# Four graph layers on one core: layer 0 loads x a second time, turned, in place of TensorE's transposes, and GpSimd forms the low half

## The chip, the core and the metric

The kernel runs on one core of a Trainium2 chip. The metric is the time of one execution on the device in microseconds; before the change it is 3392.47 us (median of 3 runs, 3390.36 to 3393.5).

## What is computed

Four layers in turn over x of 128 graphs x 64 nodes x 512 features (float32), each `x = layernorm(x + layer(x))`. Layer 0, the one that matters here, is

```python
Wi, Wj = (W[:, :Din], W[:, Din:])
mi = jnp.einsum('bkd,od->bko', x, Wi)
mj = jnp.einsum('bkd,od->bko', x, Wj)
a = adj.astype(x.dtype)
deg = a.sum(axis=1)
out = deg[None, :, None] * (mi + b) + jnp.einsum('ij,bjo->bio', a, mj)
x = _layernorm(x + out)
```

Layer 1 is a graph attention layer with four heads, an output head and a feed-forward part; layers 2 and 3 are attention layers with one head. None of them is touched.

## The kernel before

The 8192 rows of x are cut into T = 64 tiles of 128 rows (two graphs). The kernel has three stages, one after the other: layer 0 over all tiles (lines 276 to 610), the heads and the output head of layer 1, and a last stage that runs the feed-forward part of layer 1 and layers 2 and 3 as a pipeline. Between stages x goes through a scratch tensor in device memory.

Each engine has its own instruction stream, written out by hand with semaphores; every engine takes its instructions strictly in the order written. Products keep nearly float32 precision by splitting each operand into a high half (rounded to the fp32r type) and a low half (the rest): `product` (L41) runs three passes, hi x hi, hi x lo and lo x hi, on line 47. So every operand needs a hi copy and a lo subtraction.

In layer 0, for a tile t:

- SyncE loads `xt` (L378, four buffers) from device memory, and stores the result `x1` (L376). It waits for x1 of tile t before it stores it, and only then issues the load of xt for tile t + XR. It also loads `v_stage` and `a_pair` (L370, L374) for the attention vectors of later layers.
- TensorE turns the four 128x128 blocks of `xt` into the PSUM tile `turn` (`turn_x`, L566), one tile ahead. `products(t, r)` then makes the Wj product (12 passes, `wj_psum`), the Wi product (12 passes, `wi_psum`, two buffers) and the product with the adjacency (`nb_psum`, L589).
- ScalarE copies `turn` to the high half `x0T_hi` (`x_hi`, L464), then copies `wj_psum` to `wj` (L471).
- VectorE forms the low half `x0T_lo` = turn - hi (`x_lo`, L504) for tile t + 1, then z = wi_psum * deg + xb (L526), z = z + nb_psum (L530), the statistics (L204, L211), in odd tiles below 48 two multiply-and-sum instructions over `v_stage` (`junk`, L541), and then the normalised result x1 (L551).
- GpSimd forms xb = xt + db (L427), where db = deg * b0, and after the statistics of the tile two 128x1 instructions, veps and rstd (L215, L222). Between them it loads and splits the weights of layer 1 that stay in SBUF for the next stage: per pair of tiles one load issued from its own queue (L411), `split_hi` (big_hi, L415) and `split_lo` (big_lo, L420). The order in `two` is: load, xb(t), split_hi, rstd(t), xb(t+1), split_lo, rstd(t+1).

The attention vectors are formed in tiles 0 to 47, in groups of 8 tiles. On SyncE and VectorE groups 1 to 3 (tiles 8 to 31) are a loop over register values, the other groups are unrolled; on GpSimd nearly all tiles run in loops of four. GpSimd's first tile waits until db is ready (`setup_step` 7, L407, set on L517); L504 for tile 0 stands on VectorE between the first and the second piece of the split of W.

Of the kernel before, what the change touches and what calls it, by code (L numbers as in the profile page):

```python
# [5 lines left out]
F32 = mybir.dt.float32  # L6
# [6 lines left out]
P = 128  # L13
# [217 lines left out]
def gnn_stack_kernel(nc, x, adj, W0T, b0, Wh, ah, Wo, ao, w1, b1, w2, b2, gamma, beta,  # L231
# [14 lines left out]
    with ExitStack() as top:  # L246
# [29 lines left out]
        with ExitStack() as ctx:  # L276
# [3 lines left out]
            def sem(n):  # L280
                return ctx.enter_context(nc.semaphore(n))

            XR, UN = 4, 4
# [8 lines left out]
            xt = [sb(f"xt{r}", [P, D]) for r in range(XR)]  # L292
            xT = [(sb(f"x0T_hi{b}", [P, KC, P], F32R), sb(f"x0T_lo{b}", [P, KC, P], F32R)) for b in range(2)]
# [11 lines left out]
            turn = [ctx.enter_context(nc.psum_tensor(f"turn0{b}", [P, KC, P], F32)) for b in range(2)]  # L305
# [6 lines left out]
            loaded = [sem(f"loaded{r}") for r in range(XR)]  # L312
            w0_loaded = [sem(f"w0_loaded{b}") for b in range(2)]
# [5 lines left out]
            xT_done, xT_hi_ready, xT_lo_ready, wj_done, wj_ready, wi_done, nb_done = (  # L319
                sem("x0T_done"), sem("x0T_hi_ready"), sem("x0T_lo_ready"), sem("wj_done"), sem("wj_ready"),  # L320
# [9 lines left out]
            def count(t, r):  # L330

                return 16 * (t // XR) + 16 if isinstance(t, int) else 4 * (t - r) + 16
# [14 lines left out]

            @block.sync
            def _(sp):
                sp.dma_start(xt[0][:], rows(x_rows, 0)).then_inc(loaded[0], 16)  # L350
                for g in range(2):
                    sp.dma_start(adj_i[g * NODES:(g + 1) * NODES, :], adj).then_inc(small_loaded, 16)
                for k in range(2 * KC // WP):
                    piece = (k * WP + KC) % (2 * KC) * P
                    ge(sp, w0_lo_ready, k - 1)
                    sp.dma_start(w0f[k % 2], W0T[piece:piece + WP * P, :].rearrange("(c p) n -> p c n", p=P)
                                 ).then_inc(w0_loaded[k % 2], 16)
                    if k == 1:
                        sp.dma_start(db[:], b0.partition_broadcast(P)).then_inc(b0_loaded, 16)
                        for r in range(1, XR):  # L360
                            sp.dma_start(xt[r][:], rows(x_rows, r)).then_inc(loaded[r], 16)

                def step(t, r, q, G):
                    late = isinstance(G, int) and G >= HEADS
                    if q is not None and r == 0:
                        ge(sp, v_part, 2 * q)
                        for k in range(2):
                            a = ((a2d, a2s), (a3d, a3s))[G - HEADS][k] if late else ah[
                                bass.ds(G, 1), k * D:(k + 1) * D].rearrange("a o -> (a o)")
                            sp.dma_start(a_pair[:, k, :], a.partition_broadcast(P)).then_inc(pair_loaded, 16)  # L370
# [14 lines left out]
            def _(pool):  # L385
# [38 lines left out]
                def tile(t, r):  # L424
                    pool.wait_ge(loaded[r], count(t, r))
                    ge(pool, own_ready, t)
                    nc.gpsimd.tensor_tensor(xb[:], xt[r][:], db[:], ALU.add).then_inc(xb_ready, 1)  # L427

                def two(t, r, q, source, k):
# [5 lines left out]
                    tile(t + 1, r + 1)  # L435
# [3 lines left out]
                def four(k, source, before):  # L439

                    for i in range(2):
                        q = 2 * k + i + before
                        two(2 * q, 2 * i, q, source, 2 * k + i)

                four(0, Wh_rows, 0)
                with pool.Fori(1, NQ // 4) as k:
                    four(k, Wh_rows, 0)
                with pool.Fori(0, NQ // 4) as k:
                    four(k, Wo, NQ // 2)

            @block.scalar
            def _(act):
                for k in range(2 * KC // WP):
                    first = (k * WP + KC) % (2 * KC)
                    if k == 0:
                        act.wait_ge(xT_done, 1)
                        nc.scalar.copy(xT[0][0][:], turn[0][:]).then_inc(xT_hi_ready, 1)
# [3 lines left out]
                def x_hi(t, b):  # L461
                    act.wait_ge(xT_done, t + 1)
                    ge(act, wi_done, t - 1)
                    nc.scalar.copy(xT[b][0][:], turn[b][:]).then_inc(xT_hi_ready, 1)  # L464
# [17 lines left out]
            def _(dve):  # L482
# [19 lines left out]
                def x_lo(t, b):  # L502
                    dve.wait_ge(xT_hi_ready, t + 1)
                    nc.vector.tensor_tensor(xT[b][1][:], turn[b][:], xT[b][0][:].bitcast(F32), ALU.subtract  # L504
                                            ).then_inc(xT_lo_ready, 1)

                for k in range(2 * KC // WP):
# [5 lines left out]
                    if k == 0:  # L513
                        x_lo(0, 0)
# [4 lines left out]
                def step(t, r, q, G):  # L519
                    b = r % 2  # L520
                    if not isinstance(t, int) or t + 1 < T:
                        x_lo(t + 1, 1 - b)
# [38 lines left out]
            def _(pe):  # L561
                def turn_x(t, r):
                    pe.wait_ge(loaded[r % XR], count(t, r % XR))
                    ge(pe, xT_lo_ready, t - 1)
                    for c in range(KC):
                        ins = nc.tensor.transpose(turn[r % 2][:, c, :], xt[r % XR][:, c * P:(c + 1) * P], ident[:])  # L566
                    ins.then_inc(xT_done, 1)

# [25 lines left out]
                turn_x(0, 0)  # L594
                pe.wait_ge(adj_T_ready, 1)
                for r in range(UN):
                    turn_x(r + 1, r + 1)
                    products(r, r)
                with pe.Fori(1, T // UN - 1) as g:
                    t = g * UN  # L600
                    for r in range(UN):
                        if r < UN - 1:
                            turn_x(t + (r + 1), r + 1)
                        else:
                            turn_x(t + UN, 0)
                        products(t + r, r)
                for r in range(UN):
                    if r < UN - 1:
                        turn_x(T - UN + r + 1, r + 1)
# [923 lines left out]
```

## Time and profile before

| | |
|---|---|
| median of 3 runs | 3392.47 us (3390.36 to 3393.5) |
| span of the profiled execution, first to last instruction | 3390.5 us |
| TensorE (PE) busy in the span | 3273.9 us, 97% |
| VectorE (DVE) | 2186.4 us, 64% |
| GpSimd (POOL) | 1989.9 us, 59% |
| ScalarE (ACT) | 1691.7 us, 50% |
| device memory traffic | 93.09 MB read, 50.33 MB written |

The profiled execution is one run; the span is shorter than the time measured for a run by what lies around it. Busy time of an engine counts compute instructions only; matmuls are pipelined, so the durations of two that follow each other overlap, and the distance between their starts says what one costs. PEld is TensorE's weight load, SPq SyncE's queue. In a timeline each row is: start in us, duration in us, engine, line, operation, output<-inputs, count, and in brackets how long the engine had been idle before it and what ended that.

### The profile page before, as it was taken

How to read it: one execution, taken by the hardware profiler on the slowest of the kernel's cores; microseconds unless marked ns; L12 is line 12 of the kernel's file. 1: busy time of each engine (PE TensorE's matmuls, PEld its weight loads, DVE VectorE, ACT ScalarE, POOL GpSimd, SP SyncE). 2: the span in 40 equal slices, each digit the busy share in tenths (PEclk: the TensorE clock that was granted, in tenths of full speed). 3: DMA queues.
4: the chain of work that ended last, by engine and by line, in shares of the span. 5: the costliest groups of instructions: out<-in, count | busy, mean ns of one | idle time of the engine just before them, and what ended most of it. 6: DMA issues, size and time to landing. Idle time of an engine off the chain costs nothing. (4 is left out here: it accounts for less than half of the span.)

```text
span 3390.5 us, 58748 instructions
## 1 busy us (share of the span) xinstructions
PE 3273.9 (97%) x16217; PEld 2651.5 (78%) x16217; DVE 2186.4 (64%) x4753; ACT 1691.7 (50%) x4193; POOL 1989.9 (59%) x2870
## 2 busy tenths in 40 slices
PE   8999989999999999999999999996999999999997
PEld 6777768888888888888888888885777777777775
DVE  6777655555555555555555555555778877877775
ACT  2111135555555555555555555543665666666665
POOL 4555564444444444444444444433888888888886
PEclk9999999999999999999999999998999999999999
DMA  4343310000000000000000000002111111111110
GB/s 140 118 127 126 94 47 16 19 19 19 19 19 19 19 19 19 19 19 19 19 19 19 19 19 19 19 25 90 41 47 56 46 46 56 46 46 50 52 46 28
DMA packets 76527, 143.98 MB, mean 42 GB/s; under 512 B 8640, under 2 KB 8640, under 8 KB 76480
## 3 DMA queue, kind: packets, MB, share of 16 engines
q1 hardware_dynamic: 73920, 135.07, 12.1%
q0 software_dynamic: 2560, 8.39, 0.9%
q8 instruction: 17, 0.28, 0.0%
q14 instruction: 30, 0.25, 0.0%
HBM read 93.09 MB, written 50.33 MB: 42 GB/s over the span
## 5 line engine op out<-in xcount | busy, mean ns | idle before, releaser
L715 POOL TENSOR_TENSOR w_first<-xin,v_row 128x512 f32<-128x512 f32 x512 | 719.9, 1427 | 493.6 <-ACT w_first L753 482.8
L845 DVE TENSOR_TENSOR hT_lo<-hv,hT_hi 128x512 fp32r<-128x512 f32 x256 | 296.7, 1159 | 428.8 <-ACT hT_hi L771 428.8
L47 PE MATMUL whp<-big_hi,xT_hi 128*128 128x512 f32 x1024 | 422.6, 413 | 0.0
L47 PE MATMUL wop<-big_hi,hT_hi 128*128 128x512 f32 x1024 | 405.2, 396 | 0.0
L47 PE MATMUL wop<-big_hi,hT_lo 128*128 128x512 f32 x1024 | 401.0, 392 | 0.0
L47 PE MATMUL whp<-big_lo,xT_hi 128*128 128x512 f32 x1024 | 401.0, 392 | 0.0
L47 PE MATMUL whp<-big_hi,xT_lo 128*128 128x512 f32 x1024 | 400.6, 391 | 0.0
L47 PE MATMUL wop<-big_lo,hT_hi 128*128 128x512 f32 x1024 | 398.7, 389 | 0.0
L767 ACT COPY wh<-whp 128x512 f32<-128x512 f32 x256 | 149.0, 582 | 384.3 <-PE whp L47 384.3
L1139 POOL TENSOR_TENSOR g_terms<-x,g_v_row 128x512 f32<-128x512 f32 x256 | 329.0, 1296 | 5.0 <-ACT x L1219 4.9
L753 ACT ACTIVATE w_first<-w_first 128x512 f32<-128x512 f32 x512 | 319.4, 627 | 5.1 <-POOL w_first L715 5.1
L916 PE MATMUL up<-ah_turned,wh 128*128 128x128 f32 x2048 | 278.3, 279 | 14.8 <-ACT ah_turned L179 13.6
L916 PEld LDWEIGHTS up<-ah_turned,wh 128*128 128x128 f32 x2048 | 253.7, 191 | 34.3 <-issue 25.1
L761 ACT ACTIVATE ex<-up 128x512 f32<-128x512 f32 x256 | 152.9, 597 | 205.6 <-PE up L916 205.4
L161 POOL TENSOR_TENSOR ao_prob<-ao_ex,ao_inv 128x64 f32<-128x64 f32 x128 | 34.8, 293 | 350.2 <-DVE ao_inv L148 350.2
L47 PEld LDWEIGHTS whp<-big_hi,xT_lo 128*128 128x128 f32 x1024 | 192.4, 188 | 42.5
L47 PEld LDWEIGHTS wop<-big_hi,hT_lo 128*128 128x128 f32 x1024 | 192.2, 188 | 41.1
L47 PEld LDWEIGHTS wop<-big_lo,hT_hi 128*128 128x128 f32 x1024 | 192.6, 188 | 38.4
L47 PEld LDWEIGHTS wop<-big_hi,hT_hi 128*128 128x128 f32 x1024 | 192.3, 188 | 37.8
L47 PEld LDWEIGHTS whp<-big_hi,xT_hi 128*128 128x128 f32 x1024 | 193.3, 189 | 32.8 <-issue 0.4
L47 PEld LDWEIGHTS whp<-big_lo,xT_hi 128*128 128x128 f32 x1024 | 193.3, 189 | 32.4
L47 PE MATMUL bank_a<-w_hi,g_xT_hi 128*128 128x512 f32 x512 | 214.0, 418 | 2.2 <-DVE g_xT_lo L1301 1.4
(200 smaller groups left out, 8018.8 us busy)
## 6 DMA issues: line engine op xcount, KB each, us to landing
xt<-in_x SPq DMA_DIRECT2D x64, 256.0 KB, 2.7
x_scratch<-x SPq DMA_DIRECT2D x64, 256.0 KB, 2.0
xin<-x_scratch SPq DMA_DIRECT2D x64, 256.0 KB, 2.6
att_scratch<-attT SPq DMA_DIRECT2D x64, 256.0 KB, 2.0
att<-att_scratch SPq DMA_DIRECT2D x64, 256.0 KB, 2.7
x1r<-x_scratch SPq DMA_DIRECT2D x64, 256.0 KB, 3.0
out<-res SPq DMA_DIRECT2D x64, 256.0 KB, 2.0
stage<-in_L_gnn_W_heads POOLq DMA_DIRECT2D x16, 256.0 KB, 2.9
```

Source lines behind the costliest of these rows:

```text
L47: ins = nc.tensor.matmul(out, a, b, start=first and c == 0 and q == 0, stop=last and c == n - 1 and q == 2)
L161: ins = nc.gpsimd.tensor_tensor(self.prob[:, :, g, :], self.ex[:], self.inv[:, :, None].to_broadcast([P, self.heads, NODES]), ALU.mult)
L715: nc.gpsimd.tensor_tensor(terms[:, k % TR, :], xin[:], v_row[:, k, :], ALU.mult).then_inc(terms_ready, 1)
L753: nc.scalar.activation(terms[:, k % TR, :], terms[:, k % TR, :], ACT.Identity, accum_out=at.f[:, k:k + 1]).then_inc(at.f_ready, 1)
L761: nc.scalar.activation(ex[h % 2][:], up[U_HEAD[h]][:], ACT.Exp).then_inc(ex_ready, 1)
L767: nc.scalar.copy(wh[:, h, :], whp[h % 2][:]).then_inc(wh_ready, 1)
L845: nc.vector.tensor_tensor(hT[h % 2][1][:].rearrange("p c n -> p (c n)"), hv[h % 2][:], hT[h % 2][0][:].bitcast(F32).rearrange("p c n -> p ...
L916: ins = nc.tensor.matmul(up[U_HEAD[h]][:, c * P:(c + 1) * P], wh[:, h, c * P:(c + 1) * P], at.turned[:, h, :], start=True, stop=True)
L1139: nc.gpsimd.tensor_tensor(g.terms[:, k, :], x, g.v_row[:, k, :], ALU.mult).then_inc(g.terms_ready, 1)
```

## The change

The host hands the kernel a second copy of x, `x_turned`, in which every 128x512 tile has its four 128x128 blocks transposed, each row of a tile still 2 KB of contiguous memory. Layer 0 loads it into `xf` (two buffers, float32, 256 KB a tile) beside xt, whose buffers go from four to two. `turn_x`, its PSUM tiles and its semaphore go. ScalarE's hi copy reads xf. The low half moves from VectorE to GpSimd, where `x_lo(t + 1)` stands ahead of xb of tile t. SyncE issues the load of xf for tile t + 2 at the head of its step t, behind a wait for x_lo of tile t, and so behind the store of x1 and the load of xt of the step before, and ahead of a_pair and v_stage. The first low half stands on GpSimd behind its wait for `setup_step` 7. GpSimd's last four tiles are taken out of its loop.

```diff
-            XR, UN = 4, 4
+            XR, UN = 2, 4
...
             xt = [sb(f"xt{r}", [P, D]) for r in range(XR)]
+            xf = [sb(f"xf{b}", [P, KC, P]) for b in range(2)]
...
             db = sb("db", [P, D])
-            turn = [ctx.enter_context(nc.psum_tensor(f"turn0{b}", [P, KC, P], F32)) for b in range(2)]
             wj_psum = ctx.enter_context(nc.psum_tensor("wj_psum", [P, D], F32))
...
             def count(t, r):
 
-                return 16 * (t // XR) + 16 if isinstance(t, int) else 4 * (t - r) + 16
+                return 16 * (t // XR) + 16 if isinstance(t, int) else 16 // XR * (t - r) + 16
...
+            def turned_rows(t):
+
+                return x_turned[bass.ts(t, P), :].rearrange("p (c n) -> p c n", n=P)
+
             @block.sync
             def _(sp):
-                sp.dma_start(xt[0][:], rows(x_rows, 0)).then_inc(loaded[0], 16)
+                sp.dma_start(xf[0][:], turned_rows(0)).then_inc(xf_loaded[0], 16)
...
                         sp.dma_start(db[:], b0.partition_broadcast(P)).then_inc(b0_loaded, 16)
-                        for r in range(1, XR):
+                        sp.dma_start(xf[1][:], turned_rows(1)).then_inc(xf_loaded[1], 16)
+                        for r in range(XR):
                             sp.dma_start(xt[r][:], rows(x_rows, r)).then_inc(loaded[r], 16)
 
                 def step(t, r, q, G):
                     late = isinstance(G, int) and G >= HEADS
+                    if not isinstance(t, int) or t + 2 < T:
+                        sp.wait_ge(xT_lo_ready, t + 1)
+                        sp.dma_start(xf[r % 2][:], turned_rows(t + 2)).then_inc(xf_loaded[r % 2], 16)
                     if q is not None and r == 0:
                         ge(sp, v_part, 2 * q)
                         for k in range(2):
...
                                             big_hi[:, bass.ds(q, 1), :].bitcast(F32), ALU.subtract
                                             ).then_inc(big_lo_ready, 1)
 
-                def tile(t, r):
-                    pool.wait_ge(loaded[r], count(t, r))
+                def x_lo(t, b):
+                    pool.wait_ge(xT_hi_ready, t + 1)
+                    ge(pool, wi_done, t - 1)
+                    nc.gpsimd.tensor_tensor(xT[b][1][:], xf[b][:], xT[b][0][:].bitcast(F32), ALU.subtract
+                                            ).then_inc(xT_lo_ready, 1)
+
+                def tile(t, r, more=True):
+                    if more:
+                        x_lo(t + 1, 1 - r % 2)
+                    pool.wait_ge(loaded[r % XR], count(t, r % XR))
                     ge(pool, own_ready, t)
-                    nc.gpsimd.tensor_tensor(xb[:], xt[r][:], db[:], ALU.add).then_inc(xb_ready, 1)
-
-                def two(t, r, q, source, k):
+                    nc.gpsimd.tensor_tensor(xb[:], xt[r % XR][:], db[:], ALU.add).then_inc(xb_ready, 1)
+
+                def two(t, r, q, source, k, last=False):
 
                     load_block(q, source, k)
                     tile(t, r)
                     split_hi(q)
                     norm.pool_rstd(nc, pool, t, x1_ready, norm_consts)
-                    tile(t + 1, r + 1)
+                    tile(t + 1, r + 1, not last)
                     split_lo(q)
                     norm.pool_rstd(nc, pool, t + 1, x1_ready, norm_consts)
 
-                def four(k, source, before):
+                def four(k, source, before, last=False):
 
                     for i in range(2):
                         q = 2 * k + i + before
-                        two(2 * q, 2 * i, q, source, 2 * k + i)
-
+                        two(2 * q, 2 * i, q, source, 2 * k + i, last and i == 1)
+
+                x_lo(0, 0)
                 four(0, Wh_rows, 0)
                 with pool.Fori(1, NQ // 4) as k:
                     four(k, Wh_rows, 0)
-                with pool.Fori(0, NQ // 4) as k:
+                with pool.Fori(0, NQ // 4 - 1) as k:
                     four(k, Wo, NQ // 2)
+                four(NQ // 4 - 1, Wo, NQ // 2, True)
...
                     if k == 0:
-                        act.wait_ge(xT_done, 1)
-                        nc.scalar.copy(xT[0][0][:], turn[0][:]).then_inc(xT_hi_ready, 1)
+                        act.wait_ge(xf_loaded[0], 16)
+                        nc.scalar.copy(xT[0][0][:], xf[0][:]).then_inc(xT_hi_ready, 1)
...
                 def x_hi(t, b):
-                    act.wait_ge(xT_done, t + 1)
+                    act.wait_ge(xf_loaded[b], turned_count(t, b))
                     ge(act, wi_done, t - 1)
-                    nc.scalar.copy(xT[b][0][:], turn[b][:]).then_inc(xT_hi_ready, 1)
+                    nc.scalar.copy(xT[b][0][:], xf[b][:]).then_inc(xT_hi_ready, 1)
...
-                def x_lo(t, b):
-                    dve.wait_ge(xT_hi_ready, t + 1)
-                    nc.vector.tensor_tensor(xT[b][1][:], turn[b][:], xT[b][0][:].bitcast(F32), ALU.subtract
-                                            ).then_inc(xT_lo_ready, 1)
-
...
-                    if k == 0:
-                        x_lo(0, 0)
...
-                    if not isinstance(t, int) or t + 1 < T:
-                        x_lo(t + 1, 1 - b)
...
-                def turn_x(t, r):
-                    pe.wait_ge(loaded[r % XR], count(t, r % XR))
-                    ge(pe, xT_lo_ready, t - 1)
-                    for c in range(KC):
-                        ins = nc.tensor.transpose(turn[r % 2][:, c, :], xt[r % XR][:, c * P:(c + 1) * P], ident[:])
-                    ins.then_inc(xT_done, 1)
...
-                turn_x(0, 0)
...
                     t = g * UN
                     for r in range(UN):
-                        if r < UN - 1:
-                            turn_x(t + (r + 1), r + 1)
-                        else:
-                            turn_x(t + UN, 0)
                         products(t + r, r)
...
+        if name == 'x':
+            n_rows, width = a.size // a.shape[-1], a.shape[-1]
+            turned = _np.ascontiguousarray(a.reshape(n_rows // P, P, width // P, P).transpose(0, 3, 2, 1)
+                                           .reshape(n_rows, width))
+            arrays["in_x_turned"] = turned
+            args.append(nc.dram_tensor("in_x_turned", turned.shape, _mybir.dt.from_np(turned.dtype),
+                                       kind="ExternalInput").ap())
```

## Rows read from the trace of the kernel before

**Rows 1.** The page: its first line, span and instructions.

```profile
span 3390.5 us, 58748 instructions
```

**Rows 2.** Stretches of layer 0: span, busy time of each engine, PEclk, DMA share, GB/s.

```profile
80.00:240.00 160.00, 160.00 (x698) 122.59 (x697) 124.93 (x213) 26.97 (x46) 87.56 (x104) 1.00 0.38 120
...
350.00:440.00 90.00, 90.00 (x393) 68.79 (x392) 52.37 (x93) 15.26 (x26) 44.47 (x59) 1.00 0.30 96
```

**Rows 3.** Timeline of TensorE, last tiles of layer 0, line 589 alone.

```profile
432.48 1.02 PE L589 MATMUL nb_psum<-wj,adj_T 128*128 128x512 f32 x2
...
446.25 1.02 PE L589 MATMUL nb_psum<-wj,adj_T 128*128 128x512 f32 x2
...
452.71 1.02 PE L589 MATMUL nb_psum<-wj,adj_T 128*128 128x512 f32 x2
```

**Rows 4.** GpSimd's lines 1129 and 420: duration ns min/median/max, first and last start.

```profile
L1129 POOL TENSOR_TENSOR att_lo<-att,att_hi x64: 1265/1288/1829, 2319.7 to 3323.6; 128x512 fp32r<-128x512 f32 x64
...
L420 POOL TENSOR_TENSOR big_lo<-stage,big_hi x32: 1458/1472/1481, 24.2 to 451.2; 128x512 f32 x30, 128x512 fp32r<-128x512 f32 x2
```

**Rows 5.** Timeline of a pair of tiles in the loop of SyncE and VectorE.

```profile
205.48 0.75 DVE L526 SCALAR_TENSOR_TENSOR z<-wi_psum,deg,xb 128x512 f32<-128x512 f32 x1 [1.31 <-PE wi_psum L47]
206.35 0.69 DVE L530 TENSOR_TENSOR z<-nb_psum,z 128x512 f32<-128x512 f32 x1
...
209.91 0.60 POOL L411 DMA_DIRECT2D stage<-in_L_gnn_W_heads  x1
209.99 2.13 DVE L551 TENSOR_SCALAR x<-z,n_mv,n_rstd 128x512 f32<-128x512 f32 x1 [0.38 <-POOL n_rstd L222]
210.53 1.30 POOL L427 TENSOR_TENSOR xb<-xt,db 128x512 f32<-128x512 f32 x1
...
212.65 0.73 DVE L526 SCALAR_TENSOR_TENSOR z<-wi_psum,deg,xb 128x512 f32<-128x512 f32 x1
...
213.41 0.69 DVE L530 TENSOR_TENSOR z<-nb_psum,z 128x512 f32<-128x512 f32 x1
...
213.62 0.33 SPq L374 DMA_DIRECT2D v_stage<-in_L_gnn_W_heads  x1
...
215.94 1.29 POOL L427 TENSOR_TENSOR xb<-xt,db 128x512 f32<-128x512 f32 x1
216.09 1.42 DVE L551 TENSOR_SCALAR x<-z,n_mv,n_rstd 128x512 f32<-128x512 f32 x1 [1.04 <-POOL n_rstd L222]
...
217.20 1.47 POOL L420 TENSOR_TENSOR big_lo<-stage,big_hi 128x512 f32 x1
```

**Rows 6.** Timeline of an odd tile in an unrolled group.

```profile
251.27 2.15 DVE L551 TENSOR_SCALAR x<-z,n_mv,n_rstd 128x512 f32<-128x512 f32 x1 [0.38 <-POOL n_rstd L222]
...
254.31 0.44 SPq L374 DMA_DIRECT2D v_stage<-in_L_gnn_W  x1
```

**Rows 7.** DMA issues (KB each, median us to landing), and v_stage's landings.

```profile
v_stage<-in_L_gnn_W_heads SPq DMA_DIRECT2D x16, 256.0 KB, 2.9
...
DMA to landing us min/median/max: 2.7/3.0/6.5
```

**Rows 8.** Timeline of tile 9, whose first sum starts late.

```profile
81.52 0.75 DVE L526 SCALAR_TENSOR_TENSOR z<-wi_psum,deg,xb 128x512 f32<-128x512 f32 x1 [1.31 <-PE wi_psum L47]
...
85.33 0.60 POOL L411 DMA_DIRECT2D stage<-in_L_gnn_W_heads  x1
```

**Rows 9.** Timeline of tiles without sums, from 370 us.

```profile
373.62 0.55 POOL L222 TENSOR_TENSOR n_rstd<-n_veps,norm_consts 128x1 f32<-128x1 f32 x1
...
375.14 1.30 POOL L427 TENSOR_TENSOR xb<-xt,db 128x512 f32<-128x512 f32 x1
...
387.97 0.55 DVE L551 TENSOR_SCALAR x<-z,n_mv,n_rstd 128x512 f32<-128x512 f32 x1 [0.93 <-POOL n_rstd L222]
```

**Rows 10.** Timeline of the start of the kernel.

```profile
10.68 0.78 PE L47 MATMUL wj_psum<-w_hi,x0T_hi 128*128 128x512 f32 x1
...
11.03 0.48 DVE L517 TENSOR_SCALAR db<-db,deg 128x512 f32<-128x512 f32 x1
```

More of the change, by code:

```diff
@@ L228, in pool_rstd, with gnn_stack_kernel @@
                                     ).then_inc(self.shift_ready, 1)
-def gnn_stack_kernel(nc, x, adj, W0T, b0, Wh, ah, Wo, ao, w1, b1, w2, b2, gamma, beta,
+def gnn_stack_kernel(nc, x, x_turned, adj, W0T, b0, Wh, ah, Wo, ao, w1, b1, w2, b2, gamma, beta,
                      W2, a2s, a2d, W3, a3s, a3d, out):
@@ L312, in gnn_stack_kernel @@
             loaded = [sem(f"loaded{r}") for r in range(XR)]
+            xf_loaded = [sem(f"xf_loaded{b}") for b in range(2)]
             w0_loaded = [sem(f"w0_loaded{b}") for b in range(2)]
@@ L318, in gnn_stack_kernel @@
                 sem("bd_turned"), sem("adj_T_ready"))
-            xT_done, xT_hi_ready, xT_lo_ready, wj_done, wj_ready, wi_done, nb_done = (
-                sem("x0T_done"), sem("x0T_hi_ready"), sem("x0T_lo_ready"), sem("wj_done"), sem("wj_ready"),
+            xT_hi_ready, xT_lo_ready, wj_done, wj_ready, wi_done, nb_done = (
+                sem("x0T_hi_ready"), sem("x0T_lo_ready"), sem("wj_done"), sem("wj_ready"),
                 sem("wi_done"), sem("nb_done"))
@@ L330, in count, with turned_count @@
             def count(t, r):
-                return 16 * (t // XR) + 16 if isinstance(t, int) else 4 * (t - r) + 16
+                return 16 * (t // XR) + 16 if isinstance(t, int) else 16 // XR * (t - r) + 16
+            def turned_count(t, b):
+                return 16 * (t // 2) + 16 if isinstance(t, int) else 8 * (t - b) + 16
             def groups(eng, step):
@@ L593, in _ @@
                 nc.tensor.transpose(nb_psum[1][:, 0:P], adj_bd, ident[:]).then_inc(bd_turned, 1)
-                turn_x(0, 0)
                 pe.wait_ge(adj_T_ready, 1)
                 for r in range(UN):
-                    turn_x(r + 1, r + 1)
                     products(r, r)
@@ L601, in _ @@
                     for r in range(UN):
-                        if r < UN - 1:
-                            turn_x(t + (r + 1), r + 1)
-                        else:
-                            turn_x(t + UN, 0)
                         products(t + r, r)
                 for r in range(UN):
-                    if r < UN - 1:
-                        turn_x(T - UN + r + 1, r + 1)
                     products(T - UN + r, r)
```

## The prediction

> **What bounds the kernel now.** I read the page's span and slices first, then the stretches of layer 0, then its first, middle and last tiles in the timeline. The tiles of layer 0, the only part that the diff touches, are done by some 455 of 3390.5 us [rows 1, 3]. Between 80 and 440 us TensorE has no idle time, at the full granted clock; VectorE is busy 0.78 of the time while it sums the attention vectors and 0.58 after, GpSimd 0.55, ScalarE 0.17 [rows 2]. So TensorE sets the pitch of a tile: two tiles from one adj product (L589) to another are 446.25 - 432.48 = 13.77 us, 6.885 each. The last tile has no turn of a following tile in front of it, and takes 452.71 - 446.25 = 6.46 [rows 3]. That pair is the price of four transposes: 0.425 us, the slower start of the product behind them included.
>
> I time the rest from the start of VectorE's z on L526. "Even" and "odd" are t. In odd tiles 1 to 47 VectorE also runs two sums (junk, L541), and in every step from odd to even GpSimd issues the load of a weight block (L411).
>
> **What goes.** 64 x 4 transposes: 64 x 0.425 = 27.2 us if TensorE stays the bound. VectorE loses x_lo, and ScalarE's copy reads SBUF instead of PSUM (0.59 us today; no row for the new source, I take the same, as ScalarE is idle most of the time). Both engines wait before and after, so this is worth nothing by itself.
>
> The Trainium skill ("TensorE: Matmul & The Clock Gate", Part 4) gives about 275 ns for a transpose in context. By it the first term would be 64 x 1.1 = 70 us. The trace disagrees: the pitch says 0.425 for four, because they overlap.
>
> **What comes.** GpSimd forms the low half: same shapes and types as its att_lo in the last stage of the kernel, median 1.29 us [rows 4]. Its work per tile goes from 0.55 x 6.89 = 3.8 to 5.1 us, under 6.46, so its share isn't the bound. Its order is. x_lo(t+1) stands ahead of xb(t), and both stand behind rstd(t-1). VectorE's z(t) waits for xb(t), the statistics wait for z(t), and rstd(t) waits for them. That is a closed ring of GpSimd and VectorE, hidden under TensorE today, with one xb in it. Now it holds x_lo too. TensorE's two result buffers let it run ahead but don't shorten the ring.
>
> The ring, even to odd. From a z whose data is waiting to GpSimd free: 212.65 to 215.94, 3.29 us. Then x_lo 1.26 (start to start, as xb 215.94 to big_lo 217.20), then xb. VectorE's x1 (L551) asks as x_lo begins. Beside xb it lasts 1.4 to 1.5 us and ends 0.3 after it, and the GpSimd operation behind is stretched: big_lo, always behind such an x1, has 1.47 us [rows 4, 5]. I give xb that 1.47 instead of its 1.29, and 0.04 to the start of z: 6.06 us. The bounds of the stretch are 0 and 0.18; I take 0.18 as each of 32 big_lo shows it.
>
> Odd to even, with sums: z 205.48 to GpSimd free 209.91 is 4.43, since veps and rstd wait for the two sums; less 0.11, as a late z finds the adj product ready (0.76 to the next operation, 212.65 to 213.41, instead of 0.87), 4.32. Load issue 0.62, x_lo 1.27, xb 1.47, 0.04: 7.72. The pair is 13.78, and today's is 13.77 [rows 5]. In 24 of 32 pairs the ring eats all that TensorE saves. For the 12 unrolled pairs (tiles 0 to 7 and 32 to 47) I count 0.
>
> In the loop (12 pairs, tiles 8 to 31) the new load on SP's queue is late as well. SP issues it after x1's store and the xt load. An x1 of an odd tile asks while the weight load is being issued and gets in neither then nor between it and xb: 2.13 us, ending 0.29 after xb [rows 5]. Now it ends 0.29 after x_lo, at 4.32 + 0.62 + 1.30 + 0.29 = 6.53. The third DMA of a round starts 1.50 after x1 (212.12 to 213.62; here v_stage, which the x_turned load now precedes) and lands 2.9 later [rows 5, 7]: 10.93. ScalarE's hi copy 0.59 and two handoffs of 0.1 (rstd's end 215.96 to x1 216.09 is 0.13): 11.72. Then x_lo 1.26, xb 1.29 (x1 ran while GpSimd waited) and 0.1: the pair is 14.37, 0.60 over today. With landings of 2.7, the shortest, it is 14.17; of 3.9, 15.37. In three of the 12 (tiles 9, 17, 25) the first sum starts late and rstd slips in ahead: z to free is 81.52 to 85.33, 3.81 [rows 8], so 14.37 - 0.62 = 13.75, no change. 9 x 0.60 = +5.4 us. In the unrolled groups the third DMA starts 0.89 after x1 (253.42 to 254.31) [rows 6]; the copy is ready at 6.53 + 0.89 + 2.9 + 0.7 = 11.02 and GpSimd comes free at 7.72 + 3.29 = 11.01: just in time, with no slack.
>
> Without sums (tiles 48 to 63), odd to even: 3.29, at most 0.97 to the next big operation (374.17 to 375.14), 1.27, 1.29, 0.04: 6.86, as x1 gets in ahead of the issue there, 0.55 us [rows 9]. With 6.06 a pair is 12.92 at most, and TensorE's is 12.92. TensorE bounds again: 16 x 0.425 = -6.8 us.
>
> Start. The first product starts at 10.68 today. GpSimd can't begin the first low half before the bias row is ready (setup_step 7, 11.51 today, some 0.6 earlier once VectorE's x_lo is gone): 10.95 to 12.3. The product starts 1.7 us later; the later weights, which TensorE waits for within this tile, don't move by it and give some back: +1.1 us, between 0.3 and 2 [rows 10]. The end of the layer and the other layers stay as they are.
>
> **The sum.** 0 + 5.4 - 6.8 + 1.1 = -0.3 us. On the profiled span, 3390.5, that is 3390.2. The median of the runs, 3392.47, is 2.0 above the span, so the forecast is 3392.2.
>
> The Trainium skill ("SBUF — State Buffer", Who interferes with whom) has the rule that speaks against this edit: VectorE and GpSimd share a port pair by exclusive lock, a VectorE tensor_tensor with one PSUM input stays out of it, while every SBUF read of GpSimd takes it. The trace agrees as far as x1's 0.55 against 1.5 and 2.13 go. By its "Issue order, not op shape, decides who blocks", x1 would come ahead of x_lo in odd tiles too, as it asked first, and the loads would be in time, as in the second rival; the row of 2.13 speaks against that.
>
> **Rivals.**
> - TensorE bounds throughout, the ring being shorter than I add up. For: every busy share is under the pitch. Against: 7.72 is made of rows and would have to come below 6.86. -27.2 + 1.1: 3366.4. Chance 0.13.
> - Light ring: xb isn't stretched (2 x 0.18 a pair) and the loads are in time, 24 pairs of 13.42: -8.4 - 6.8 + 1.1 = -14.1, 3378.4. Chance 0.15.
> - Slower, x1 behind both: after the issue of the weight load x1 waits for x_lo and xb together, as it waited for issue and xb [rows 5]. It ends at 7.79, and the x_turned load follows it: pairs of 14.87 unrolled, 15.63 in the loop, 15.01 in the three. 12 x 1.10 + 9 x 1.86 + 3 x 1.24 = +33.6, with -6.8 + 1.1 +27.9: 3420.4. It decides as soon as x1 ends more than 6.5 us after z. Against: between xb and big_lo x1 does get in. Chance 0.12.
> - Slower, late landings: each tile moves 256 KB more, and the DMA share of 0.38 [rows 2] goes to some 0.5. A landing 1 us later than 2.9 costs 1 us in each of 24 pairs: 3392.2 + 24 = 3416.2. v_stage's 2.7 to 6.5 says that it can be [rows 7]. Chance 0.12.
> - The change does something else than it says, or other layers move by over 5 us: 0.03.
>
> **How the numbers follow.** The forecast, 3392.2 with chance 0.45, has 3384 to 3401 as its own range (stretch, landings of 2.7 to 3.2, start). The range of 3374 to 3418 leaves out the first rival and about half of the third, some 0.19. 0.2%, 6.8 us, is about what a measurement can tell from no change. Faster: 0.13 + 0.15 + a tenth of the forecast, 0.33. Slower: 0.24 + an eighth of it, 0.30. Same: 0.37.
>
> **What would show it.** TensorE should have idle time ahead of wj products between 30 and 350 us, some 0.5 to 1 us a pair, and none from 360 on, with a pitch of 6.46. A z should start within 0.15 us of xb's end, not wait for wi_psum. x1 of odd tiles should end 0.3 after x_lo. In tiles 8 to 31 x_lo of even tiles should wait 0.4 to 0.6 us for the hi copy, and that for the x_turned DMA. I am wrong if the pitch is 6.46 before tile 48, if x1 lasts until after xb, or if x_turned lands later than 3.2 us after its issue.

## The result, and the profile after

The changed kernel takes 3409.55 us (median of 4 runs, 3404.87 to 3415.11), the kernel before, run beside it, 3392.98: a ratio of 1.0049, 95% interval 1.0035 to 1.0063. It is slower by some 17 us, where -0.3 was forecast. In both profiled executions the last z of layer 0 starts 16.0 us later (469.01 instead of 452.96) and the span is 16.5 longer, so the loss lies in layer 0. The page after, and two stretches of layer 0 (columns as in [rows 2]):

```profile
span 3407.0 us, 58302 instructions
```

```profile
80.00:240.00 160.00, 148.64 (x581) 106.83 (x580) 98.96 (x181) 24.97 (x44) 110.52 (x123) 1.00 0.47 153
350.00:440.00 90.00, 85.84 (x343) 63.51 (x342) 51.56 (x89) 14.69 (x26) 61.48 (x73) 1.00 0.42 137
```

TensorE was busy for all 160 us of the first stretch [rows 2] and now has 11 us of idle time there. No other engine is full. What holds it is in the waits from 60 to 460 us (engine and line, what was waited for: us in total, times, longest):

```profile
ACT x0T_hi L487 <- DMA xf<-in_x_turned: 324.0, 55, 10.4
DVE z L540 <- POOL xb L448: 104.5, 40, 3.8
...
POOL x0T_lo L440 <- ACT x0T_hi L487: 24.8, 20, 1.9
```

z waits for xb as forecast. But x_lo waits for the hi copy, and that one for the x_turned load. An odd tile (z at 259.17) and the even one ahead of it, in an unrolled group, from the timeline:

```profile
248.53 3.35 DVE L565 TENSOR_SCALAR x<-z,n_mv,n_rstd 128x512 f32<-128x512 f32 x1
...
252.01 0.75 DVE L540 SCALAR_TENSOR_TENSOR z<-wi_psum,deg,xb 128x512 f32<-128x512 f32 x1
...
252.96 0.34 SPq L377 DMA_DIRECT2D xf<-in_x_turned  x1
...
254.79 0.56 POOL L222 TENSOR_TENSOR n_rstd<-n_veps,norm_consts 128x1 f32<-128x1 f32 x1
...
255.93 0.62 ACT L487 CAST x0T_hi<-xf 128x512 fp32r<-128x512 f32 x1 [9.36 <-DMA xf<-in_x_turned]
256.62 1.26 POOL L440 TENSOR_TENSOR x0T_lo<-xf,x0T_hi 128x512 fp32r<-128x512 f32 x1 [1.27 <-ACT x0T_hi L487]
257.85 1.29 POOL L448 TENSOR_TENSOR xb<-xt,db 128x512 f32<-128x512 f32 x1
259.17 0.75 DVE L540 SCALAR_TENSOR_TENSOR z<-wi_psum,deg,xb 128x512 f32<-128x512 f32 x1 [3.23 <-POOL xb L448]
...
263.49 0.60 POOL L424 DMA_DIRECT2D stage<-in_L_gnn_W_out  x1
263.56 3.35 DVE L565 TENSOR_SCALAR x<-z,n_mv,n_rstd 128x512 f32<-128x512 f32 x1 [0.38 <-POOL n_rstd L222]
264.10 1.28 POOL L440 TENSOR_TENSOR x0T_lo<-xf,x0T_hi 128x512 fp32r<-128x512 f32 x1
265.32 1.29 POOL L448 TENSOR_TENSOR xb<-xt,db 128x512 f32<-128x512 f32 x1
267.05 0.75 DVE L540 SCALAR_TENSOR_TENSOR z<-wi_psum,deg,xb 128x512 f32<-128x512 f32 x1
```

Read the last five rows first. I take the start of a row as the moment when the instruction asks, and what x1 has over its 0.55 us as waiting. x1 of the odd tile asks 0.07 us into the issue of the weight load and ends at 266.91, 0.30 after xb: it waited for the issue, for x_lo and for xb. In [rows 5] the same x1 took 2.13 and ended behind one operation. The pair before shows what this costs: x1 ends at 251.88, SyncE stores it, loads xt and issues the x_turned load only at 252.96; the copy ends at 256.55 and GpSimd has stood idle for 1.27 us. From 252.01 to 259.17 it is 7.16 us; the forecast's ring has 6.06.

It isn't so in every odd tile. Of the 24 odd tiles below 48, 17 have an x1 of 3.08 to 3.91 us. In 13 of them it ends some 0.3 after xb; in four (tiles 1, 5, 29 and 47, 3.90 or 3.91) big_hi follows xb without a gap and x1 ends 0.3 after that. In the other 7, tiles 3, 7, 11 and so on to 27, it gets in during the issue, which then lasts longer:

```profile
219.14 0.74 POOL L424 DMA_DIRECT2D stage<-in_L_gnn_W_heads  x1
...
219.22 0.55 DVE L565 TENSOR_SCALAR x<-z,n_mv,n_rstd 128x512 f32<-128x512 f32 x1 [0.38 <-POOL n_rstd L222]
```

The account by the distance from z to z, in us for a pair of tiles. Tiles 0 to 7, 8 to 31, 32 to 47, and 48 to the last:

| | 0-7 | 8-31 | 32-47 | 48-63 |
|---|---|---|---|---|
| before | 13.77 | 13.80 | 13.76 | 13.69 |
| forecast, change over the stretch | 0 | +5.4 | 0 | -6.8 |
| after | 14.61 | 14.52 | 15.05 | 12.88 |
| after, change over the stretch | +3.4 | +8.6 | +10.3 | -6.1 |

With -0.2 at the start, instead of +1.1, that is +16.0.

### The profile page after: what moved, and what is told of

Same layout as the page of the kernel before. It is cut to its first block and busy times, and to the rows that moved or that the text cites. A ratio compares the mean times of both kernels' runs of the same rounds, so it can differ in the third digit from the quotient of the medians.

```text
span 3407.0 us, 58302 instructions
## 1 busy us (share of the span) xinstructions
PE 3257.3 (96%) x15961; PEld 2620.9 (77%) x15961; DVE 2143.0 (63%) x4689; ACT 1690.2 (50%) x4193; POOL 2066.9 (61%) x2934
## 5 line engine op out<-in xcount | busy, mean ns | idle before, releaser
L487 ACT CAST x0T_hi<-xf 128x512 fp32r<-128x512 f32 x63 | 39.1, 621 | 361.5 <-DMA xf<-in_x_turned 359.2
```

The lines of the kernel that those rows point to most:

```text
L487: nc.scalar.copy(xT[b][0][:], xf[b][:]).then_inc(xT_hi_ready, 1)
```

## The experiments

All are edits of the changed kernel, but for load_only, which is one of the kernel before. Each ratio is to the kernel before, run beside it on the same chip. Pair and steps are z to z; even to odd (e-o) and odd to even (o-e) are medians over the steps from z of tile 32 to z of tile 47. Of x1 the median over the odd tiles below 48 is given; where it is long in some and short in others, one median for each kind.

| | median us | ratio to before | 95% interval | pair 8-31 | pair 32-47 | e-o | o-e | x1 of odd tiles |
|---|---|---|---|---|---|---|---|---|
| after | 3409.55 | 1.0049 | 1.0035-1.0063 | 14.52 | 15.05 | 7.13 | 7.81 | 3.35 / 0.55 |
| early | 3389.90 | 0.9987 | 0.9978-0.9996 | 13.72 | 13.89 | 6.06 | 7.81 | 3.35 / 0.55 |
| swap | 3383.46 | 0.9967 | 0.9956-0.9979 | 13.76 | 13.65 | 5.60 | 8.24 | 3.36 / 0.55 |
| low_dve | 3381.34 | 0.9962 | 0.9948-0.9975 | 13.42 | 13.49 | 6.51 | 6.97 | 2.13 |
| turns_back | 3417.13 | 1.0066 | 1.0053-1.0080 | 14.50 | 15.17 | 7.09 | 7.82 | 3.36 / 0.55 |
| hw_load | 3376.93 | 0.9960 | 0.9946-0.9973 | 13.32 | 13.28 | 6.32 | 6.99 | 1.49 |
| swap_hw_load | 3371.12 | 0.9940 | 0.9926-0.9953 | 13.10 | 13.10 | 6.62 | 6.45 | 1.5 |
| x1_psum | 3386.95 | 0.9988 | 0.9979-0.9997 | 13.75 | 13.94 | 6.44 | 7.44 | 0.81 |
| swap_x1_psum | 3381.84 | 0.9966 | 0.9952-0.9980 | 13.46 | 13.55 | 7.06 | 6.45 | 0.81 |
| no_sums | 3371.01 | 0.9935 | 0.9921-0.9948 | 12.91 | 12.86 | 6.06 | 6.62 | 0.55 |
| load_only | 3393.85 | 1.0004 | 0.9995-1.0013 | 13.80 | 13.76 | 6.70 | 7.07 | 2.13 |
| swap_hw_early | 3372.28 | 0.9943 | 0.9929-0.9956 | 13.11 | 13.11 | 6.64 | 6.45 | 1.5 |

**early: is it the load?** The x_turned load of a tile goes out a step sooner, so that no x1 of an odd tile stands in front of the one that is wanted next.

```diff
-                    if not isinstance(t, int) or t + 2 < T:
-                        sp.wait_ge(xT_lo_ready, t + 1)
-                        sp.dma_start(xf[r % 2][:], turned_rows(t + 2)).then_inc(xf_loaded[r % 2], 16)
+                    if not isinstance(t, int) or t + 3 < T:
+                        sp.wait_ge(xT_lo_ready, t + 2)
+                        sp.dma_start(xf[1 - r % 2][:], turned_rows(t + 3)).then_inc(xf_loaded[1 - r % 2], 16)
...
+                sp.wait_ge(xT_lo_ready, 1)
+                sp.dma_start(xf[0][:], turned_rows(2)).then_inc(xf_loaded[0], 16)
                 groups(sp, step)
```

> The changed kernel with the x_turned load issued one tile earlier by SyncE (tile t + 3 instead of t + 2 at the head of step t, into the buffer that x_lo of tile t + 1 has just left). Ring theory: the ring of x_lo and xb remains, only its wait for the hi copy goes; even to odd falls from 7.1 to about 6.1, odd to even stays at 7.6 to 7.9, so 48 tiles have pairs of 13.7 to 13.9 (before: 13.77), the last 16 are 6.5 us faster: 3386 to 3389. Rival (the late load is all there is, without it TensorE would bound): 3366. Rival (loads don't matter, x1 behind both operations alone costs it): stays at 3405 to 3410.

All the loss over before goes. A pair in the timeline:

```profile
202.75 1.27 POOL L442 TENSOR_TENSOR x0T_lo<-xf,x0T_hi 128x512 fp32r<-128x512 f32 x1
204.00 1.46 POOL L450 TENSOR_TENSOR xb<-xt,db 128x512 f32<-128x512 f32 x1
...
205.50 0.75 DVE L542 SCALAR_TENSOR_TENSOR z<-wi_psum,deg,xb 128x512 f32<-128x512 f32 x1 [1.18 <-POOL xb L450]
...
213.16 0.75 DVE L542 SCALAR_TENSOR_TENSOR z<-wi_psum,deg,xb 128x512 f32<-128x512 f32 x1 [2.68 <-POOL xb L450]
```

GpSimd goes from x_lo to xb to z with no gap from 202.75 on, both z wait for xb, and even to odd is 6.06 in every stretch, as forecast; odd to even is 7.66 in the loop by the median, where 7.72 was forecast. x1 is as long as in the changed kernel (17 times over 3 us, 7 times 0.55, in the same tiles). So the size of the ring was right, and a long x1 costs most of what it costs by way of the load behind it; what is left is some 0.26 us in the step, by which z stands behind it on VectorE (in the loop 7.93 with a long x1, 7.66 with a short one, 7.31 in tiles 9, 17 and 25, where rstd slips in ahead).

**hw_load: is it the issue on GpSimd that makes x1 wait?** ScalarE issues the weight load in place of GpSimd.

```diff
-                    pool.dma_start(stage[:], source[bass.ts(k, P), :]).then_inc(stage_loaded, 16)
...
+                    act.dma_start(stage[:], source[bass.ts(k, P), :]).then_inc(stage_loaded, 16)
```

> The changed kernel, order x_lo then xb kept, with the weight block's load issued by ScalarE ahead of its even steps instead of by GpSimd. Ring theory: the issue, 0.62 us, leaves the odd-to-even part, and x1 of odd tiles asks as x_lo starts, so it ends 0.3 us after x_lo and not behind both; the loads are then in time too: odd to even 4.32 + 1.27 + 1.47 + 0.04 = 7.10, even to odd 6.06, pairs of 13.16 against 13.77: 3393 - 24 x 0.61 - 6 = 3372. Rival (x1 waits until GpSimd pauses whatever came before): x1 of odd tiles still 2.8 us or more, loads late, pairs above 13.8, 3390 or more.

```profile
205.00 1.27 POOL L436 TENSOR_TENSOR x0T_lo<-xf,x0T_hi 128x512 fp32r<-128x512 f32 x1
205.06 1.48 DVE L571 TENSOR_SCALAR x<-z,n_mv,n_rstd 128x512 f32<-128x512 f32 x1 [0.38 <-POOL n_rstd L222]
206.22 1.47 POOL L444 TENSOR_TENSOR xb<-xt,db 128x512 f32<-128x512 f32 x1
...
207.73 0.75 DVE L546 SCALAR_TENSOR_TENSOR z<-wi_psum,deg,xb 128x512 f32<-128x512 f32 x1 [1.19 <-POOL xb L444]
```

x1 asks 0.06 into x_lo, now a compute operation, and gets in between x_lo and xb, in all 24 odd tiles; xb is stretched from 1.29 to 1.47. That is what the forecast assumed of x1 in general. The step from odd to even also loses the 0.62 of the issue (6.99 to 7.10). Even to odd is 6.1 to 6.4, over the 6.06 of the ring, since x_lo still waits up to 0.5 us for the hi copy and that for the load, hence 3376.9 where 3372 was expected.

The Trainium skill ("SBUF — State Buffer", SBUF: two separate sides) warns of a DMA issued from GpSimd's queue beside a VectorE operation in a 2-port mode, and advises to issue it from ScalarE or SyncE. It speaks of the issue being held up; the issue of 0.74 instead of 0.60 under an x1 of 0.55 agrees, and the advice pays here (1.0049 to 0.9960). The larger effect of this kernel, an x1 held up from the issue to the end of two later operations, isn't in it.

**swap: x_lo behind xb.** xb, for which z waits, comes first.

```diff
-                    if more:
-                        x_lo(t + 1, 1 - r % 2)
...
+                    if more:
+                        x_lo(t + 1, 1 - r % 2)
```

(The two lines move below the instruction of xb.)

> The changed kernel with one thing turned round: GpSimd forms xb of tile t first and x_lo of tile t + 1 behind it, where it otherwise stands idle during the statistics. Ring theory (the order x_lo, xb, statistics, rstd is what sets the pitch): x_lo leaves the ring, z to z falls to TensorE's 6.46 us in all 64 tiles, 27 us under the kernel before: 3366. Rival A, the third 256 KB load of a tile is what hurts (landings and SyncE's queue): the load and its place in SyncE's queue are as in the changed kernel, so it stays above 3400. Rival B, GpSimd's added 1.3 us beside VectorE (their shared port) is what hurts, wherever it stands: 3390 to 3410.

```profile
249.34 3.90 DVE L565 TENSOR_SCALAR x<-z,n_mv,n_rstd 128x512 f32<-128x512 f32 x1 [0.38 <-POOL n_rstd L222]
249.88 1.30 POOL L446 TENSOR_TENSOR xb<-xt,db 128x512 f32<-128x512 f32 x1
251.13 1.27 POOL L440 TENSOR_TENSOR x0T_lo<-xf,x0T_hi 128x512 fp32r<-128x512 f32 x1
...
253.37 0.75 DVE L540 SCALAR_TENSOR_TENSOR z<-wi_psum,deg,xb 128x512 f32<-128x512 f32 x1
```

xb is done at 251.18, but z starts at 253.37: it stands behind x1 on VectorE, and x1 waits for xb, x_lo and big_hi (252.34 to 252.95) and ends 0.29 later. So it is in 5 of the 17 tiles with a long x1; in the other 12 it ends 0.3 after x_lo. Only 0.33% is won where some 0.8% was expected. But x1's wait isn't what sets the pair: swap_x1_psum, in which it is gone, is no faster (0.9966). What does is worked out there.

**swap_hw_load: both.** The edits of swap and hw_load together: x_lo stands behind xb, and ScalarE issues the weight load.

> xb ahead of x_lo, and the weight load issued by ScalarE: the two changes together. If x1 of odd tiles gets the port behind the first operation, the ring is 4.32 + 1.29 + 0.04 at most and TensorE bounds all 64 tiles with 6.46: 3366. Rival (x1 still waits behind xb and x_lo in odd tiles): 3380.

With x1 at 1.5 us z no longer waits for x_lo. With swap_hw_early, which is the same within the noise, this is the fastest kernel that does the whole work, 0.60% under before and so ahead of both kernels. 3366 was expected. Odd to even is 6.45, TensorE's own pitch; even to odd is 6.62 to 6.73.

**swap_hw_early: is that last 0.17 a late load?** To swap_hw_load the edit of early is added.

> xb ahead of x_lo, weight load issued by ScalarE, and the x_turned load one tile earlier. In swap_hw_load pairs are 13.1 where TensorE's are 12.92. If the rest is the late hi copy, which ScalarE makes ahead of its wj copy (at 258.3 and 258.8 there), the pairs fall to 12.92 and the time by 24 x 0.16 = 4 us to 3367. Rival (it is something else in the odd tiles): stays at 3371.

It isn't: the pitches are the same within 0.02. In the timeline TensorE waits for x_lo itself:

```profile
255.58 1.47 POOL L438 TENSOR_TENSOR x0T_lo<-xf,x0T_hi 128x512 fp32r<-128x512 f32 x1
...
256.19 1.02 PE L604 MATMUL nb_psum<-wj,adj_T 128*128 128x512 f32 x2
...
257.15 0.47 PE L47 MATMUL wj_psum<-w_hi,x0T_hi 128*128 128x512 f32 x1
257.45 0.40 PE L47 MATMUL wj_psum<-w_lo,x0T_hi 128*128 128x512 f32 x1
```

x_lo ends at 257.05 and the next tile's first product starts at 257.15; elsewhere that product starts some 0.46 after the adj product (397.80 to 398.26 in swap_hw_load), here 0.96. Of these 0.50 only 0.17 is lost: the second pass starts 1.26 after the adj product here, and 1.09 in the tile before (249.73 to 250.82), where the first pass had been early and lasted longer. The 0.18 that the waiting x1 adds to x_lo is of the size of the loss. What makes x_lo so late is a second ring, in the rows of swap_x1_psum.

**x1_psum: an x1 that doesn't contend.** The second z goes to PSUM, and the statistics and x1 read it there, so x1 reads its tile from PSUM and not from SBUF.

```diff
-                    nc.vector.tensor_tensor(z[:], nb_psum[b][:], z[:], ALU.add).then_inc(z_ready, 1)
+                    nc.vector.tensor_tensor(zp[:], nb_psum[b][:], z[:], ALU.add).then_inc(z_ready, 1)
```

> The changed kernel with the sum z + nb_psum written to PSUM, from where the statistics and x1 read it: x1 then has one PSUM input and no second port. Port theory: x1 takes about 0.7 us in every tile, whatever GpSimd does, nothing stretches xb, the loads are in time: odd to even 4.32 + 0.62 + 1.27 + 1.29 + 0.04 = 7.5, even to odd 5.9, pairs of 13.4: 3393 - 24 x 0.35 - 6 = 3378. Rival (x1 waits for something else than the port, the order of its semaphores for example): its 3.35 us stay and the time is 3405 or more.

```profile
210.46 0.60 POOL L425 DMA_DIRECT2D stage<-in_L_gnn_W_heads  x1
210.53 0.81 DVE L566 TENSOR_SCALAR x<-zp,n_mv,n_rstd 128x512 f32<-128x512 f32 x1 [0.38 <-POOL n_rstd L222]
211.08 1.28 POOL L441 TENSOR_TENSOR x0T_lo<-xf,x0T_hi 128x512 fp32r<-128x512 f32 x1
212.30 1.29 POOL L449 TENSOR_TENSOR xb<-xt,db 128x512 f32<-128x512 f32 x1
```

x1 is 0.81 in every tile, starts into the issue and x_lo without waiting, and xb isn't stretched. Odd to even is 7.44 to 7.53 (7.5 expected). Even to odd is 5.9 to 7.25 instead of 5.9, and 3387 us came where 3378 was expected: the x_turned landings have a median of 3.2 us, against 2.9 to 3.0 in hw_load and early. In tiles 32 to 43 the step follows the landing: the hi copy of the even tile starts 4.2 to 5.2 us after the load was issued, and the step is 6.08 with the shortest of these and 7.25 with the longest. That the landings are late because the transfers of a pair now bunch is my reading; no run isolates it.

**swap_x1_psum: the same with xb first.** The edits of swap and x1_psum together.

> xb ahead of x_lo, and x1 out of PSUM. Port and ring theory: the ring holds neither x_lo nor a wait of x1, odd to even is 4.32 + 0.62 + 1.29 + 0.04 = 6.3, TensorE bounds with 6.46 in all 64 tiles: 3366. Rival: as swap alone, 3383, if what held the odd tiles there was not x1's wait.

Odd to even is TensorE's 6.45, even to odd 7.05 to 7.16, in which z waits for wi_psum. 3381.8 came instead of some 3366, so the rival put on record with this run ("as swap alone, 3383") held. ScalarE's hi copy waits for the x_turned load (265 us in all between 60 and 460), but that isn't the wait that counts: in odd tiles x_lo starts 2.2 to 4.7 us after the hi copy has ended. From z of an odd tile, which started at 242.78, to z of the next odd one:

```profile
247.25 0.60 POOL L425 DMA_DIRECT2D stage<-in_L_gnn_W_out  x1
247.87 1.31 POOL L447 TENSOR_TENSOR xb<-xt,db 128x512 f32<-128x512 f32 x1
249.11 1.28 POOL L441 TENSOR_TENSOR x0T_lo<-xf,x0T_hi 128x512 fp32r<-128x512 f32 x1
...
250.50 0.47 PE L47 MATMUL wj_psum<-w_hi,x0T_hi 128*128 128x512 f32 x1 [0.42 <-issue]
...
256.43 0.75 DVE L541 SCALAR_TENSOR_TENSOR z<-wi_psum,deg,xb 128x512 f32<-128x512 f32 x1 [2.84 <-PE wi_psum L47]
```

There is no slack in it: each row starts within some 0.1 us of the end of the one that it waits for, and z waits for wi_psum. It is a second ring, through GpSimd, TensorE and VectorE, which stands in no forecast: z, statistics, sums and rstd, load issue, xb, then x_lo for the next odd tile, that tile's 24 passes on TensorE, and its z. By medians over tiles 33 to 47 it is 4.97 to xb, 1.26 to x_lo, 1.26, 0.10 to the first pass and 5.93 to z, 13.52 in all, and the pair is 13.55. In swap its steps follow as closely, and the distance from z of an odd tile to the next is 13.49 to 13.91. Without the issue on GpSimd and with the longer x_lo, in swap_hw_load and swap_hw_early, it is 4.34 + 1.25 + 1.46 + 0.10 + 5.93 = 13.08 (measured pairs 13.10 and 13.11). So with xb first this ring, and no longer the one of GpSimd and VectorE, sets the pair. It is worked out from the rows of four kernels; no run was made for it.

**low_dve: the low half on VectorE, no transposes.** The `x_lo` of GpSimd moves back to VectorE behind x1, with xf as its input.

```diff
-                    nc.gpsimd.tensor_tensor(xT[b][1][:], xf[b][:], xT[b][0][:].bitcast(F32), ALU.subtract
+                    nc.vector.tensor_tensor(xT[b][1][:], xf[b][:], xT[b][0][:].bitcast(F32), ALU.subtract
```

> The second load of x and the missing transposes stay as in the changed kernel; only the low half goes back to VectorE, at its old place, now with both inputs in SBUF. Ring theory: GpSimd has one xb in the ring as before the change, TensorE bounds with 6.46: about 3367; a VectorE operation with two SBUF inputs may wait for GpSimd or hold it up, up to 1.3 us beside 0.68, and still fits: at most 3375. Rival A (the loads): above 3400.

```profile
213.36 1.47 POOL L433 TENSOR_TENSOR big_lo<-stage,big_hi 128x512 f32 x1
...
213.61 1.78 DVE L519 TENSOR_TENSOR x0T_lo<-xf,x0T_hi 128x512 fp32r<-128x512 f32 x1
```

With both inputs in SBUF the subtraction, 0.68 us from PSUM before, takes 1.78 beside big_lo. So it is in the steps from even to odd; in the others, below tile 48, nothing runs on GpSimd beside it, and it takes 0.68 from SBUF too. The pair is 13.4 to 13.5, only 0.3 under the 13.77 of before, z follows right behind x_lo, and 3381 us came where 3367, at most 3375, was expected. So even without GpSimd's new work, dropping the transposes doesn't bring their 27.2 us: the second load, which replaces them, puts both operands of the subtraction in SBUF, and VectorE's part of the ring grows.

**turns_back: what are the transposes worth now?** TensorE does four transposes of a constant block at the place of before; nothing reads them.

```diff
+                    for c in range(KC):
+                        nc.tensor.transpose(turn[b][:, c, :], same_graph[:], ident[:])
```

> The changed kernel with four transposes per tile put back on TensorE ahead of the products, on constant data into PSUM tiles that nobody reads, so that they wait for nothing. Ring theory: TensorE waits in tiles 0 to 47, so nothing changes there; in tiles 48 to 63 it is the bound and gets 0.425 us more: 3409.6 + 6.8 = 3416. Rival (TensorE is still the bound of every tile, at a slower rate): 3409.6 + 27 = 3437.

By the medians it costs 7.6 us over the changed kernel, by the ratios to the kernel before 5.8, and their intervals overlap; the stretches of the two traces say more: the last z starts 7.25 us later; 0.65 of it is there at the first z, at most 0.06 a tile comes in tiles 0 to 47, and 0.39 a tile from 48 on. Its adjacency product in the tail, then that of the changed kernel:

```profile
420.91 1.02 PE L599 MATMUL nb_psum<-wj,adj_T 128*128 128x512 f32 x2
...
427.80 1.02 PE L599 MATMUL nb_psum<-wj,adj_T 128*128 128x512 f32 x2
```

```profile
391.22 1.02 PE L596 MATMUL nb_psum<-wj,adj_T 128*128 128x512 f32 x2
...
397.68 1.02 PE L596 MATMUL nb_psum<-wj,adj_T 128*128 128x512 f32 x2
```

6.89 against 6.46: the price of 0.43 a tile holds where TensorE bounds.

**no_sums: the ring with its sums out.** Two clears of 128x1 take the place of the two multiply-and-sum instructions of odd tiles, so the attention vectors are left out.

```diff
-                            nc.vector.tensor_tensor_reduce(
+                            nc.vector.memset(v_sums[:, r // 2, k:k + 1], 0.0).then_inc(v_part, 1)
```

> The changed kernel without VectorE's two sums per odd tile: each is replaced by a clear of its result (this leaves the attention vectors of layers 1 to 3 out of the computation, at equal work there). Ring theory: z to GpSimd free in odd tiles falls from 4.32 to 3.29, odd to even to 6.6 to 6.9 as tiles 49 to 63 have it, pairs to TensorE's 12.92 everywhere, if x1 of odd tiles gets in ahead of the issue as it does in tiles 48 to 63: 3367. If it waits behind both operations all the same, the late load brings even to odd to 7.1 and pairs to 13.9: 3387. Rival (the sums don't matter for the ring): 3409.

Odd to even falls by 0.8 to 1.2 us, to 6.6 and 6.9 in turn, and the pitch is TensorE's 6.45 in all stretches but the first. x1 asks at the very start of the issue or up to 0.44 ahead of it and is 0.55 in all but one odd tile. So two things go at once, the sums' part of the ring and x1's wait; as the step is still 7.4 to 7.7 in x1_psum and with the short x1 of early, which have the sums and no wait of x1, the sums are the part of the ring that lets it exceed TensorE.

**load_only: does the extra traffic cost anything?** To the kernel before one more load of 256 KB a tile is added, into a buffer that nothing reads by then.

```diff
+                    if not isinstance(t, int) or t + 1 < T:
+                        sp.wait_ge(xf_loaded, 16 * t + 16)
+                        sp.dma_start(xf, turned_rows(t + 1)).then_inc(xf_loaded, 16)
```

> The kernel before with nothing changed but one more load of 256 KB a tile on SyncE's queue, x_turned into SBUF that nobody reads, issued at the place where the change issues it. Ring theory: traffic by itself costs nothing, landings rise by 0.3 us at most, 3393 as before, within 3. Rival (the added traffic or its place in SyncE's queue is a cost of its own): 3400 or more.

Nothing measurable: 1.0004, 0.9995 to 1.0013, with the DMA share of the stretch 80 to 240 us at 0.50, as against 0.38 [rows 2].

## Why the prediction was wrong, point by point

- **The failed step: x1 of odd tiles.** "Now it ends 0.29 after x_lo, at ... 6.53." In 17 of 24 odd tiles, where it asks in the issue of the weight load, it ends 0.30 after xb or later: 7.16 to 7.79 after z in 13 of them (259.17 to 266.91, 7.74, in the rows above), and 8.2 to 8.3 in the four in which it waits for big_hi too. This is the third rival, which said 7.79 and had a chance of 0.12. The row of 2.13 [rows 5] allowed two readings: x1 waits for one operation behind the issue, or for all that follow without a gap. There was only one behind it in the kernel before, so the row couldn't tell, and I took the cheaper reading by likeness to x1 in even tiles. hw_load shows that the likeness held only without an issue. Nor did x1 always miss the issue before, as I wrote: in tile 7 of the kernel before it got in (0.55, issue 0.74), which the prediction leaves out.
- **The unrolled pairs, counted at 0 with "no slack".** They lost 3.4 + 10.3 us. The rival's 14.87 for a pair is 15.05 in tiles 32 to 47. Its sum of 3420.4 was too high for two reasons. 7 x1 got in early, five of them in the loop. And in the loop the x_turned load starts 1.06 to 1.08 us after x1 (1.23 behind tiles 9, 17 and 25), not the 1.50 that I took from the place of v_stage. So from z of an odd tile with a long x1 to z of the next odd one it is 15.03 to 15.08 there (15.60 once), where the rival had 15.63, and 14.4 to 14.7 from tiles 9, 17 and 25, where it had 15.01; the mean pair is 14.52.
- **The ring, 6.06 and 7.72**: right in size, the first also in its terms, the second by luck. early gives 6.06 with xb stretched to 1.46, as assumed. Odd to even its medians are 7.66 in the loop and 7.81 in tiles 32 to 47, but xb is 1.29 there, not 1.47: what fills the place of the 0.18 is the z that stands behind a long x1, or, where x1 gets in, an issue of 0.74 instead of 0.60. No light ring all the same. Of what a pair of the changed kernel has over 13.78 in tiles 32 to 47, by the medians, 1.07 is from even to odd (the load) and 0.09 from odd to even.
- **The loop, +5.4**: +8.6. Nearer than its terms were: the load starts 0.43 sooner after x1 than the 1.50 of the sum, which by itself would leave 9 x 0.17 = +1.5; seven long x1 made up for that, also in tiles 9, 17 and 25, for which I had counted no change.
- **Tiles 48 to 63, -6.8**: -6.1, pair 12.88 against 12.92. Right. turns_back gives the same price.
- **The start, +1.1**: -0.2. The first product starts 1.39 us later, at 12.07 (1.7 forecast), but the twelve wj passes take 4.25 us instead of 5.21 (10.68 to 15.89 before): the starts of passes are 0.43 us apart until 15.52 in the kernel before and until 14.77 in this one, and 0.23 later on, so that the late start meets fewer of the slow ones (six behind the first pass instead of eleven). A wait of 0.5 us for weights goes as well (17.05 to 17.79 before). Granted clock is 1.00 in both; what slows the early passes no run shows.
- **Landings**: right by the median, 2.9 to 3.0 us from the issue of x_turned (2.7 to 5.3). The late-landing rival falls, with load_only.
- **The transposes, 70 us or 27.2**: the trace disagrees with 70, as the prediction has it, but not with what one transpose lasts, which is 0.273 us (median of 256 before). Only their plain sum doesn't hold, as the pitch has 0.425 for four.
- **TensorE throughout, 3366.4**: only reached, nearly, with the sums out (3371.0) or with the issue moved and xb first (3371.1). There the ring through GpSimd, TensorE and VectorE, 13.08, stands in its way; the prediction has no such ring.
- **The sum.** The range held the time, but with the sign on the side that I gave 0.30. Had the unrolled groups been counted with the loads on x1's real end, the change would have read slower: "just in time, with no slack" should have weighed on the chances of that rival.

## What to carry to other kernels

When work leaves the bounding engine, add up the closed chains of the others, engine queue by engine queue; here one of 13.8 us for two tiles took the place of TensorE's 12.92, and no busy share showed it. Look also for a chain that passes through the bounding engine: once the first was shortened, such a one of 13.1 to 13.5 bounded, and runs that were to bring 3366 stopped at 3371 to 3383. A new load issued behind a store inherits every delay of what is stored: issue it a step sooner, which was worth 0.6% here. And a row that shows a wait behind one operation says nothing on a wait behind two: where the change puts a second one there, price both readings, and keep DMA issues off the queue of GpSimd where VectorE's SBUF operations come beside them.

## What the runs showed of the hardware that I had not expected

- A VectorE tensor_scalar from SBUF to SBUF (x1, 0.55 us alone) that asks 0.07 to 0.09 us into a DMA issue on GpSimd (0.35 in tiles 9, 17 and 25) waits, in 17 of 24 cases, for the issue and both 128x512 operations behind it (3.35 us; 3.08 with the later ask), and in four of these for a third one that follows without a gap (3.90); 0.06 us into a compute operation it waits for that one alone (1.48). The other 7 times it gets in during the issue, which takes 0.74 instead of 0.60. The moment of asking doesn't decide: it is 0.07 to 0.09 in these 7 too. The place in the program goes with it: they are tiles 3, 7, 11, 15, 19, 23 and 27, the second pair of each round of four on GpSimd, in this kernel as in early, turns_back and swap, but not tile 31 or a later one. What decides stays open. The Trainium skill ("SBUF — State Buffer", Who interferes with whom) has it that whoever issues first gets the shared port pair for the whole instruction; x1 had issued ahead of x_lo and xb and got it after both, so here the measurement decides.
- A GpSimd operation behind such a waiting x1 takes 1.47 instead of 1.29 us, and once x1 reads PSUM, it doesn't (x1_psum).
- The same subtraction on VectorE is 0.68 us with one PSUM input; with two SBUF inputs it is 0.68 or 0.69 in 29 of 64 tiles, nearly always with nothing beside it on GpSimd, and 1.77 to 1.80 in 29, beside big_lo (low_dve). By the same section two SBUF inputs contend with a GpSimd operation that reads SBUF; the trace agrees.
